# Score row products on 64 rows, two heads at once, four in a burst through four PSUM banks

## The reference, cut to what matters

```python
q, k, v = (proj(Wq), proj(Wk), proj(Wv))
scores = jnp.einsum('bhsd,bhtd->bhst', q, k) * scale
scores = jnp.where(mask[None, None, :, :], -jnp.inf, scores)
attn = jax.nn.softmax(scores, axis=-1)
out = jnp.einsum('bhst,bhtd->bhsd', attn, v)
```

## Time and profile before

| | |
|---|---|
| median of 3 runs | 1164.3 us (1163.31 to 1166.56) |
| profiled execution, span | 1162.1 us, from the first to the last instruction |
| PE busy | 1122.4 us, 97% |
| DVE, ACT, POOL busy | 770.8, 803.1, 512.6 us |
| attention, steady part | about 60 to 560 us of the span |
| mean granted TensorE clock | 0.996 of full speed |

### The profile page before, as it was taken

One profiled execution on the slowest core, in us unless ns is written; L12 is line 12 of the kernel. 1 busy time (PEld: TensorE's weight loads), 2 busy tenths in 40 slices (PEclk: granted clock), 3 DMA queues, 4 the chain that ended last, 5 costly groups with the idle time before them and its releaser, 6 DMA issues.

```text
span 1162.1 us, 23399 instructions
## 1 busy us (share of the span) xinstructions
PE 1122.4 (97%) x7520; PEld 763.4 (66%) x7520; DVE 770.8 (66%) x2265; ACT 803.1 (69%) x1752; POOL 512.6 (44%) x837
## 2 busy tenths in 40 slices
PE   8899999999999999998989999999999999999988
PEld 4333434434334343342418999998999999999968
DVE  4877777787887878878745434355555555667747
ACT  2578888787787877877786756655666666666645
POOL 8424135583755837657462365354222223222220
PEclk8999999999999999999999999999999999999999
DMA  8665638367384572843837488856566766723536
GB/s 220 193 195 189 219 100 250 124 215 231 119 257 138 198 235 94 242 157 133 286 101 269 115 309 306 267 120 133 155 193 190 213 193 179 226 48 70 164 91 217
DMA packets 101616, 213.64 MB, mean 184 GB/s; under 512 B 10917, under 2 KB 71341, under 8 KB 93046
## 3 DMA queue, kind: packets, MB, share of 16 engines
q1 hardware_dynamic: 86038, 192.42, 51.1%
q0 software_dynamic: 14304, 18.69, 9.0%
q10 hardware_dynamic: 1152, 1.05, 0.4%
HBM read 239.28 MB, written 74.29 MB: 270 GB/s over the span
## 4 chain that ended last, share of the span: by engine, by line
PE 46%; ACT 3%; issue 1%; DVE 1%; POOL 1%; DMA 1%; another core or an unknown queue 0%; ACTq 0%; POOLq 0%
PE bank L1084 38%; PE bank L1247 1%; PE bank L1189 1%; PE bank L1099 1%; ACT pt L1355 1%; PE bank L1170 1%; DMA x<-yout,rows 1%; PE bank L1113 1%; PE bank L1174 1%; PE bank L1207 1%; PE bank L1282 0%; PE bank L1155 0%; PE bank L1227 0%; ACT full L1433 0%
## 5 line engine op out<-in xcount | busy, mean ns | idle before, releaser
L1628 DVE CUSTOM_DVE_ANT_0 junk<-bank,mneg 128x512 bf16<-128x512 f32 x512 | 333.0, 683 | 119.0 <-PE bank L1155 116.3
L1355 ACT ACTIVATE pt<-bank 128x512 f32<-128x512 f32 x512 | 301.0, 594 | 67.8 <-PE bank L1170 29.7
L1975 POOL DMA_INDIRECT x<-yout,rows x78 | 122.8, 1574 | 292.9 <-ACT yout L1438 249.6
L1084 PE MATMUL bank<-hid,w 128*128 128x256 f32 x1872 | 242.7, 286 | 4.2 <-DVE hid L1776 3.8
L1084 PEld LDWEIGHTS bank<-hid,w 128*128 128x128 f32 x1872 | 229.3, 190 | 6.0 <-issue 4.8
L1776 DVE TENSOR_TENSOR hid<-full,hid 128x256 fp32r<-128x256 f32 x312 | 133.3, 431 | 135.3 <-ACT full L1433 126.8
L1428 ACT ACTIVATE hid<-bank,biases 128x256 fp32r<-128x256 f32 x312 | 149.4, 479 | 91.6 <-PE bank L1084 88.0
L1433 ACT ACTIVATE full<-bank,biases 128x256 f32<-128x256 f32 x312 | 148.7, 477 | 0.0
L1174 PE MATMUL bank<-mneg,identb 128*128 128x512 bf16 x386 | 146.9, 381 | 0.0
L1084 PE MATMUL bank<-rowsT,w 128*128 128x256 f32 x936 | 122.9, 284 | 0.9 <-issue 0.9
L1084 PE MATMUL bank<-w,hid 128*128 128x256 f32 x936 | 121.9, 283 | 1.5 <-DVE hid L1776 1.5
(11 more groups left out here) (184 smaller groups left out, 1445.2 us busy)
## 6 DMA issues: line engine op xcount, KB each, us to landing
w<-split_weights SPq DMA_DIRECT2D x80, 1024.0 KB
w<-split_weights SPq DMA_DIRECT2D x40, 2048.0 KB
split_weights<-w_parts SPq DMA_DIRECT2D x64, 512.0 KB, 3.8
w_parts<-in_W SPq DMA_DIRECT2D x64, 256.0 KB, 4.3
split_parts<-parts SPq DMA_DIRECT2D x28, 384.0 KB, 2.6
rows<-routed SPq DMA_DIRECT2D x39, 258.0 KB, 3.4
stacks<-split_parts SPq DMA_DIRECT2D x36, 256.0 KB, 5.2
qst<-split_parts SPq DMA_DIRECT2D x24, 256.0 KB, 5.3
```

Of the source, the lines that this page charges most:

```text
L1084: product = T.matmul(ps, w[p], x[q], start=(k == 0 and n == 0), stop=(k == len(weights) - 1 and n == 2))
L1355: A.activation(pt[n % len(pt)][:, :], bank[3 + n % 2][:, :], ACT.Exp, scale=float(D) ** -0.5).then_inc(exped.sem, 1)
L1628: V.tensor_tensor_reduce(junk[n % 2][:, :], bank[n % 3][:, :], mneg[:, 0, st, :], 1.0, FLOOR, ALU.add, ALU.max, rowmax[gi % 2][:, hh, st:s ...
L1975: G.indirect_dma_start(x2_dram, bass.IndirectOffsetOnAxis(ap=rows[j % NS][:, tt, E + 1:E + 2].bitcast(U32), axis=0), yout[j % NY][:, tt], ...
```

## The change

1. Row products use four of the six pairs of parts, 64 contraction rows (`KR`). The stacks are laid out anew: the first two heads of each group have these rows on partitions 0 to 63, the last two on 64 to 127 (`slot_of`, `pair_rows`). The column products of the last two heads contract over all 128 partitions, some of which hold zeros.
2. From group 2 on the four row products of a step are issued together at its start (`rows`), heads 0, 2, 1, 3, into banks 0, 1, 2 and 7. Each waits for the reduction of the fourth product back. DVE's order within the step stays one tile per head. In groups 0 and 1 they are issued one at a time (`one_row`), the first two heads of both groups first.
3. The four column products of a step follow without row products between them. The values steps stand directly behind the burst in the odd steps `k`, no longer after the third head of the even ones.
4. All other users have bank 6 alone while row products run. `bank_free` and `bank_read` hold chain steps and `todo` items back until the bank is likely to be free; one item may now stand after the second head of an even step (not a projection), and one after steps 1 to 3. Values and output work enter the list a little earlier or at other places.
5. Transfers: 24 instead of 12 for the stacks of a batch, two instead of one for the maxima of a group. Constants: four fills of 2048 floats in place of one of 8192 bf16 numbers, for each of two buffers.

Only the core is shown. Left out are the callers' signal counts (twice the transfers), the yields of `bank()` in `chain`, the second transfer of the maxima, the fills, and the permutation of the weights on the host.

```diff
@@ -34,14 +36,22 @@
-FIRST_PROJECTS = range(3, 7)
+FIRST_PROJECTS = range(2, 6)
 PAIRS = [(0, 0), (1, 0), (0, 1), (1, 1), (0, 2), (2, 0)]
 KQ = len(PAIRS) * D
+ROW_PAIRS = 4
+KR = ROW_PAIRS * D
+ROW_HEADS = (0, 2, 1, 3)
+ROW_BANKS = (0, 1, 2, 7)
 STACK_STEPS = 3
 MASKED = -7.0 * 2.0 ** 125
+TWO_MINUS_ONES = struct.unpack("<f", struct.pack("<I", 0xBF80BF80))[0]
...
@@ -126,7 +141,51 @@
-def chain(b, out):
+def slot_of(h):
+    g, hh = divmod(h, GH)
+    return hh // 2 * (H // 2) + g * (GH // 2) + hh % 2
+def pair_rows(half, r):
+    if r < ROW_PAIRS:
+        first, step = half * KR + r, ROW_PAIRS
+    else:
+        first, step = (KR, KR // 2)[half] + r - ROW_PAIRS, len(PAIRS) - ROW_PAIRS
+    return slice(first, first + (D - 1) * step + 1, step)
+def shift_rows_of(half):
+    return slice(0, SHIFTS) if half else slice(KQ, KQ + SHIFTS)
+def bank_free(order):
+    cols = 0
+    for step in reversed(order):
+        if step[0] in ONE_BANK:
+            return False
+        if step[0] in ("layer1", "layer2", "layer3"):
+            return True
+        cols += step[0] == "col"
+        if cols == APART:
+            return True
+    return True
+def bank_read(order):
+    last = next(step[0] for step in reversed(order) if step[0] in ONE_BANK + ("logits", "ranks"))
+    return last not in ("gate", "place")
+def chain(b, out, attention=False):
+    def bank():
+        while attention and not bank_free(out.order):
+            yield
...
@@ -285,22 +347,31 @@
     out.extend(value_steps(0))
+    first_rows = [(i, hh, st) for n in range(2) for i in range(2) for st in range(ST) for hh in (2 * n, 2 * n + 1)]
     for i in range(GROUPS + 3):
         b = i // NG
         if i % NG == 0 and b + 1 < B:
             todo[:0] = project_steps(b + 1)
-        if i % NG == 2 and b + 1 < B:
-            todo += value_steps(b + 1)
         if i == 2:
             todo += [("prepare",), ("modulation",)]
         for k in range(ST):
+            if i % NG == 2 and k == 1 and b + 1 < B:
+                todo += value_steps(b + 1)
             if i % NG == 2 and k == 2 and 0 <= b - 1 < B - 1:
                 todo += finish_steps(b - 1)
-            g, kt = (i - 2, k - 2) if k > 1 else (i - 3, ST - 2 + k)
+            if 2 <= i < GROUPS:
+                out.append(("rows", i, k))
+            g, kt = (i - 2, 0) if k == 3 else (i - 3, 2)
+            if k % 2 and 0 <= g < GROUPS:
+                out.append(("weigh", g, kt))
+                out.append(("weigh", g, kt + 1))
             for n in range(GH):
-                if i < GROUPS:
-                    out.append(("row", i, n, k))
-                if k == 0 and n == 0 and 0 <= i - 1 < GROUPS:
+                if i < 2:
+                    found = first_rows[(i * ST + k) * GH + n]
+                    out.extend((("one_row", *found), ("row", *found)))
+                elif i < GROUPS:
+                    out.append(("row", i, ROW_HEADS[n], k))
+                if n == 0 and ((i, k) == (1, 2) or k == 0 and 2 <= i <= GROUPS):
                     out.append(("split_maxima", i - 1))
...
@@ -309,9 +380,6 @@
                         out.append(("layer1", 0, m))
-                if n == 2 and k % 2 == 0 and 0 <= g < GROUPS:
-                    out.append(("weigh", g, kt))
-                    out.append(("weigh", g, kt + 1))
                 if i * ST + k in FIRST_PROJECTS and n == 1 and i < 2:
...
@@ -329,8 +397,10 @@
                     chains.pop(0)
-            if k == 1 and 0 <= i - 1 < GROUPS:
-                out.append(("maxima_rows", i - 1))
+                if n == 1 and k % 2 == 0 and i >= 2 and todo and todo[0][0] != "project" and bank_read(out.order):
+                    work_off()
+                if (i, k, n) == (1, 2, 2) or (k, n) == (0, 3) and 2 <= i <= GROUPS:
+                    out.append(("maxima_rows", i - 1))
             n, step = divmod((i - 1) * ST + k, 2)
...
@@ -350,9 +420,8 @@
                     out.append(("fetch_weights", layer, 1))
-            for _ in range(2 if len(todo) > 12 else 1):
-                if todo and i >= 2:
-                    work_off()
+            if todo and i >= 2 and (k or i > GROUPS) and bank_read(out.order):
+                work_off()
     out.extend(todo)
...
@@ -748,7 +817,14 @@
     misc_users = [s for s in order if s[0] in misc_stages and s[:2] != ("project_v", 0)]
-    misc_place = {s: n for n, s in enumerate(misc_users)}
+    row_steps = [n for n, s in enumerate(order) if s[0] in ("one_row", "rows")]
+    turn_place = {s: n for n, s in enumerate(order)}
+    misc_home, last_user = {}, {}
+    for n, s in enumerate(misc_users):
+        home = 6 if row_steps[0] < turn_place[s] < row_steps[-1] else 6 + n % 2
+        misc_home[s], last_user[home] = (home, last_user.get(home)), s
+        if turn_place[s] < row_steps[0]:
+            before_rows_user = last_user.get(7)
     col_place = {at: n for n, at in enumerate(cols_at)}
...
@@ -931,8 +1009,10 @@
                     for r in range(n, len(PAIRS), STACK_STEPS):
-                        start((qst, kst)[qk][b % 2][r:KQ:len(PAIRS), :, :].rearrange("d (a h) s -> d a (h s)", a=2),
-                              split_dram[b, qk, PAIRS[r][qk]].rearrange("(a d h) s -> d a (h s)", a=2, d=D)).then_inc(dma_stack[qk], 16)
+                        for half in range(2):
+                            start((qst, kst)[qk][b % 2][pair_rows(half, r), half * (H // 2):(half + 1) * (H // 2), :],
+                                  split_dram[b, qk, PAIRS[r][qk]][half * P:(half + 1) * P, :].rearrange("(d h) s -> d h s", d=D)
+                                  ).then_inc(dma_stack[qk], 16)
             elif name == "project_v":
...
@@ -1084,6 +1168,18 @@
+        def row_product(gi, hh, st):
+            b, half, at_slot = gi // NG, hh // 2, slot_of(gi % NG * GH + hh)
+            n = row_place[gi, hh, st]
+            if n >= len(ROW_BANKS):
+                pe.wait_ge(*max_found.at(rows_at[n - len(ROW_BANKS)]))
+            elif ROW_BANKS[n] == 7:
+                pe.wait_ge(*evicted(before_rows_user))
+            stacks_loaded(pe, b, half)
+            rows = slice(half * KR, (half + 1) * KR)
+            T.matmul(bank[ROW_BANKS[n % len(ROW_BANKS)]][:, :], qst[b % 2][rows, at_slot, st * P:(st + 1) * P],
+                     kst[b % 2][rows, at_slot, :], start=True, stop=True).then_inc(row_scored.sem, 1)
         def side_stage(step):
...
@@ -1145,18 +1241,16 @@
                 T.matmul(ps[0:B, :], condS[:, :], wc, start=True, stop=True).then_inc(modulated.sem, 1)
-            elif name == "row":
-                gi, hh, st = at
-                b, h = gi // NG, gi % NG * GH + hh
-                n = row_place[gi, hh, st]
-                if n >= 3:
-                    pe.wait_ge(*max_found.at(rows_at[n - 3]))
-                stacks_loaded(pe, b, h // (H // 2))
-                T.matmul(bank[n % 3][:, :], qst[b % 2][0:KQ, h, st * P:(st + 1) * P], kst[b % 2][0:KQ, h, :],
-                         start=True, stop=True).then_inc(row_scored.sem, 1)
+            elif name == "one_row":
+                row_product(*at)
+            elif name == "rows":
+                gi, st = at
+                for hh in ROW_HEADS:
+                    row_product(gi, hh, st)
             elif name == "col":
                 gi, kt, hh = at
-                b, h = gi // NG, gi % NG * GH + hh
+                b, at_slot = gi // NG, slot_of(gi % NG * GH + hh)
+                stack = slice(0, P) if hh // 2 else slice(0, KQ + SHIFTS)
                 n = col_place[gi, kt, hh]
...
@@ -1164,10 +1258,10 @@
                     pe.wait_ge(*(exped.at(cols_at[n - 2]) if n >= 2 else v_ready.at((0, ST - 1))))
-                pe.wait_ge(dma_mrow[gi % 2], 16 * (gi // 2 + 1))
+                pe.wait_ge(dma_mrow[gi % 2], 2 * 16 * (gi // 2 + 1))
                 pe.wait_ge(constants_made, CONSTANTS)
                 limit = seed or (gi, kt, hh) in cleared.value
-                product = T.matmul(ps[:, :], kst[b % 2][0:KQ + SHIFTS, h, kt * P:(kt + 1) * P], qst[b % 2][0:KQ + SHIFTS, h, :],
+                product = T.matmul(ps[:, :], kst[b % 2][stack, at_slot, kt * P:(kt + 1) * P], qst[b % 2][stack, at_slot, :],
                                    start=not seed, stop=limit, skip_group_check=seed)
...
@@ -1625,12 +1719,13 @@
                     dve.wait_ge(*max_split.at((gi - 2,)))
-                V.tensor_tensor_reduce(junk[n % 2][:, :], bank[n % 3][:, :], mneg[:, 0, st, :], 1.0, FLOOR, ALU.add, ALU.max,
+                V.tensor_tensor_reduce(junk[n % 2][:, :], bank[ROW_BANKS[n % len(ROW_BANKS)]][:, :], mneg[:, 0, st, :], 1.0, FLOOR, ALU.add, ALU.max,
                                        rowmax[gi % 2][:, hh, st:st + 1]).then_inc(max_found.sem, 1)
             elif name == "split_maxima":
                 gi, = at
-                found = rowmax[gi % 2][:, :, :]
-                first_part, second_part = (m2[gi % 2][:, :, k * GH:(k + 1) * GH].rearrange("p s h -> p h s") for k in range(SHIFTS))
```

(21 more changed lines are left out.)

22 lines of the change are left out of this document (13 added, 9 removed).

## The result

The changed kernel takes 1234.8 us (1230.93 to 1236.97, four runs) where the one before takes 1163.9 (1163.31 to 1166.56): a ratio of 1.060, 95% interval 1.058 to 1.063. It is slower by 70.8 us. The forecast was 46 us slower: right in direction, and the time lies inside the range, but a third of the loss, 25 us, was not foreseen, and the upper end of the range, 1243, is only 8 us away.

A forecast was written before the change was run, and what follows sets the result against it. TensorE, busy 97% of the span, was taken as the bound. Per group -1.16 + 3.2 - 1.1 + 0.4 + 0.2 = +1.5 us; 30 groups +45, start +1: 1164.3 + 46 = 1210 us, range 1136 to 1243.

The forecast's parts named there:

- The mechanism: Column products back to back wait for ACT's exponentials and seeds: 0.48 us per odd step, 1.12 per even, 3.2 a group.
- PE's busy share: Sign in the profile after: TensorE's busy share in 60 to 560 us falls from 98 to some 85%.
- The saving of PE: Row products paired at 0.22 us, as values quads overlap; burst with boundaries 0.64 us against 0.88; 1.16 us less a group.
- rival 2: Row products: pairs don't overlap, each costs 0.44 us, 53 us more, 1263 us; chance 0.07.
- Rival 1: Column waits get filled by other work while PE's saving stands: faster, 1142 us; chance 0.32.
- The DVE term: Even steps: DVE's four row tiles need 3.6 to 4.3 us against 3.3; 0.4 us a group, bounds 0 and 1.
- The steady part: Attention groups in regular running: terms sum to +1.5 us a group.
- "I take 0": One bank for all other users instead of two: users mostly a step apart, so no cost charged.
- rival 3: The single bank becomes the bound: some 20 users a batch wait 0.5 us each, 75 us, 1285 us; chance 0.03.
- The start: First groups: 32 row tiles bound by DVE at 0.61 us each as before; later maxima in group 0 cost 1 us.
- The tail: Last groups without row products: cited for the existing pace of 0.65 us a head; no extra cost charged.
- The clock: Granted clock stays 1.00 despite PE's gaps, as in 560 to 604 us; nothing charged.

The follow-up runs named there:

- run 1: Changed kernel with the values steps put back after the third head of the even steps, over the seed of the fourth head; 1200.9 us.
- run 2: Changed kernel without seeds in even steps, the fourth head's mask being a product on PE instead; 1205.7 us.
- run 4: Changed kernel with each burst of four row products cut into two pairs, ahead of the first and third heads; 1208.1 us.
- run 6: Changed kernel with the edits of run 1 and run 4 together; 1185.9 us.
- run 9: Kernel before the change, only product order altered from group 2 on: row products of heads 0 to 2 together, head 3 before the fourth column product; 1214.2 us.
- run 8: run 4 with three row banks and two banks in turn for all other users; 1186.1 us.
- run 11: Changed kernel with the edits of run 6 and run 8 together; 1179.7 us, ratio 1.013 to the kernel before.

## Why the prediction was right

**The mechanism** was right and is shown: the pace of two column banks through ACT takes over once no row product stands between. Runs 1, 2, 4 and 6 take its parts away one by one, and run 9 puts it into the kernel before. In the pair of steps shown the times came out to 0.01 us (2.64 and 2.01 us). PE's busy share fell less than the 98 to 85% given as a sign, to 90%: a recorded product hides 0.16 us of each of some hundred waits.

**The saving of PE** came out as worked out: pairs at 0.22 us, and a burst with both boundaries at 0.63 us beside the 0.64 charged.'s quads were a good neighbour; rival 2 is out.

**Rival 1** (waits filled) is out: the batch grew by 8.3 us, where the rival had it under 73. Its working has a slip: with a third of the 3.2 us left (1.07 of waits against 1.16 saved) the time would be 1161 us, not 1150. The 12 us for the transfers of a batch are one too: 16 issues of 0.68 us are 10.9. No term of the sum hung on either. **The DVE term**, 0.4 a group, was rather too large: halving the reduction gave 0.2. The forecast had said that DVE waits less for rows in even steps; over the span it waits more before its reductions, 155 us for 119.

**The steady part** was sized +37.5 us for groups 3 to 27, and took +47.3. What was missing there is one term, "I take 0" for the single bank: with a second bank, the six batches of run 4 take 14.0 us less (run 8), of which up to 5.1 can be clock. That spans the 9.8; the other terms were right or a little large, DVE's among them. The reasoning "a projection's eviction by ACT and DVE is over in some 1.5 us" looked at one user. The costly one was another: the turned maxima wait up to 1.8 us for ACT's copy of x1, which stands behind exponentials and seeds in ACT's order, and behind them all of PE's order waits. So rival 3 was half true. Its 0.5 us for each of 20 users didn't happen; one place in a batch did.

**The start** was charged 1 us, plus 1.5 for group 2, and took +10.3. "There the 32 tiles are bound by DVE" is the step that failed, and with it the nothing taken for the single bank there. With one bank, each chunk of a projection waits until DVE has subtracted from the chunk before it (`rest`, L1687), and the row products stand behind it in PE's order. PE's timeline of the changed kernel, then DVE's (a second chunk waits 1.57 us at 35.52, a third 1.36 at 39.83):

```profile
30.01 2.97 PE L1226 MATMUL bank<-xT,wqk 128*128 128x512 f32 x4 [1.36 <-DVE rest L1687]
```

```profile
28.04 0.69 DVE L1722 CUSTOM_DVE_ANT_0 junk<-bank,mneg 128x512 bf16<-128x512 f32 x1 [2.19 <-PE bank L1180]
```

DVE is idle for over 2 us, for PE. Run 8 gives 4.5 us of it back. The clock is half for 13.7 us more than before in this part, which can be up to 6.8 us of the 10.3; the rest was not taken apart.

**The tail** was charged nothing and took +6.9. In the trace 36 column products stand between the last reduction and the first expert product, 27 before; nine at the two-bank pace of 0.65 us are 5.9. The pipeline is not deeper; columns still run two groups behind rows. Three of the nine are there because the last burst stands ahead of the columns of its step. The other six ran before the change while DVE, 4.6 us behind PE's last row product, was still reducing; now it is 2.0 us behind. The run with a third column bank took 25.3, nearly the old time (25.1).

**The clock** was charged nothing. It stands at half for 20 us of the first 55 (7 before), and in nine more stretches of 3.4 us (one before). Half of the 51 us at the lower level is 25.6, of the 10 before 5.1: at most 20.5 us, which lie inside the terms above and not beside them. It is an upper bound, since waits are not shortened by a faster clock. The short window 560 to 604 from which I argued had the gaps of a column bank, 0.4 us, and not one of 1.8. But long waits are not the whole of it: the profiled execution of run 11 has no wait of PE over 0.8 us from 60 to 560 us and still four stretches at half clock. How much is real loss stays open too. The four executions of run 11's kernel differ by 7.4 us where their clocks allow 8, while in the rest of the program two such stretches more, 3.4 us at most, came with +0.9. What brings the lower clock about stays open.

The sum: 46 predicted; steady part +9.8, start +7.8, groups 28 to 31 -2.6 (6.0 charged), tail +6.9, rest +0.9. That is 68.8 us; the spans differ by 68.8, the medians by 70.8.

## What to carry to other kernels

When two engines pass a small number of banks back and forth, the work of a third kind that stands between is not in the way; it fills the time in which the bank comes back. Before grouping such work, write down the round of the bank (product, exponential, seed, next product) and count what covers it in the new order, in each kind of step; moving the values step by one head cost 40 us here. Then count what the grouping saves if it is done in small pieces instead: here a pair with its two boundaries took 0.42 us for 0.44. And a shared bank is not sized by its average user but by the latest read-out, which stands behind other work of the reading engine, with everything that is queued in order behind the next user.

## What was not expected of the hardware

- Two products on different 64-row halves start within 0.01 us of each other, and each half takes its next one 0.22 us later. The order of issue made no difference to the burst (0.54 us either way). The halves are concluded from the starts.
- Changing between 64-row products and full or column-strip ones shows as 0.31 us from the last pair to the next kind, 0.09 more than between products of one kind. That is the size the values step had already in the earlier trace rows.
- In the changed kernel four of five waits of PE of 1.8 us have a stretch of 3.4 us at a granted clock of 0.50 beside them, beginning within 0.4 us of the wait's end. In run 11's kernel such stretches came with no wait over 0.8 us. The same kernel was granted a mean clock from 0.981 to 0.988 in four executions.
